# Two attention layers: the next batch's input is requested before the store and load of the second key group

## The chip, the cores and the metric

The kernel runs on one core of a Trainium2 chip. The time is the device time of one launch in microseconds (us). Lower is better. The engines are TensorE (PE in the profile, its weight loads PEld), VectorE (DVE), ScalarE (ACT), GpSimd (POOL) and SyncE (SP). SP only issues DMAs here, in program order, and all of the kernel's DMAs are issued by it.

## The reference

The input x is 8 batches of 256 channels by 32 x 32 positions (1024 tokens), float32. Two layers follow one another:

```
xn  = (x - mean_c(x)) / sqrt(var_c(x) + 1e-5) * gamma     # layer norm over the 256 channels
q, k, v = split(w_qkv @ xn)                               # 8 heads of 32 rows
a   = softmax(q^T k * 32^-0.5 + bias[head])               # 1024 x 1024 for each head
x1  = w_out @ (v a^T) + x                                 # end of layer 0
f, g, h = Wf @ x1 + bf, Wg @ x1 + bg, Wh @ x1 + bh        # f, g of 32 rows, h of 256
out = gamma1 * (h softmax(f^T g)) + x1                    # end of layer 1
```

The bias is a table over relative positions that a small network computes once.

## The kernel before

The program is written engine by engine, with semaphores between the engines. The Python functions only unroll it. For each of the 8 batches `b` there are two groups `g` of four heads, and each group has two phases.

- **Rows** (32 steps, `A_TILES`): PE makes a 128 x 1024 tile of the scores (lines 622 and 623), DVE adds the bias and finds the row maximum (line 1066), ACT takes the exponential and its row sum (line 840). Only the sums are kept.
- **Columns** (32 steps, `SN`): PE makes the scores again, turned round and with the row shifts folded in as two more rows of the operands (line 643), DVE adds the bias (1080), ACT takes the exponential (857), and PE multiplies with v (670).

Beside these steps runs all the rest, by tables of (step, kind, argument): `side_0` for the rows of group 0, `column_0` for its columns, and so on. An entry is done by each engine right behind its main work of that step, so an engine that waits in such an entry holds up its next tiles too. On PE row tiles are issued from step 3 on (`LEAD`), each ahead of its step's entries.

In the rows of group 0 of batch b the entries hold, in this order: the q of group 1 (steps 3 to 8), v (4 to 11), the k of group 1 (steps 11 to 16: four products on PE at line 446, `high_k` on ACT at 745, `low_k` on DVE at 945), the output projection of the batch before (513, 963), and then the layer norm of batch b + 1:

- step 18 `sum_x` on POOL (line 877): adds the two channel halves of xn into the buffer `st`;
- steps 22 and 23 `mean` on PE (line 460), a product of `st` with a constant matrix; step 23 `centre` on DVE (937); step 24 `square` on ACT (728), into `st`; step 25 `sum_squares` on POOL (880);
- steps 28 and 29 `var` on PE (line 460 again), step 30 `rstd` on ACT (737), and `norm` on POOL (886) in the columns that follow.

The buffer `st` (128 x 2 x 1024) is shared. It holds the q or k that has just been split in a high and a low part, until SP has stored it to DRAM (`through_dram`, line 338), from where it is loaded in another layout (lines 351 and 365). So `sum_x` waits for two things (lines 875 and 876): the second store of k of this batch has landed (`k_stored`), and x of the next batch has landed in `xn` (`x_loaded`). x can be requested only when the old xn has been read to the end, by v (`v_mm`) and by the products of k (`qk_mm`).

What SP issues in one batch is in the function `element` at line 403: q store and loads of group 1 (404, 405), k store and loads of group 1 (406, 407), x of the next batch (412), the shift rows (`shift_to_stack`), k and q of the next batch's group 0, the result of the batch before and this batch's x for the residual.

Of the kernel before, what the change touches and what calls it, by code (L numbers as in the profile page):

```python
# [25 lines left out]
def two_layer_attention(nc, x, gamma, w_qkv, w_out, w0, b0, w1, b1, w2, b2,  # L26
# [24 lines left out]
    with ExitStack() as ctx:  # L51
# [133 lines left out]
        def need(eng, name, b, n):  # L185
            value = b * per_batch[name] + n
            if value > 0:
                eng.wait_ge(SEMS[name], value)
# [111 lines left out]
        def split(g, t, half=NHALF - 1):  # L300


            return (1 - t) * NHALF + half + 1 if g == 0 else 2 * NHALF + t + 1
# [4 lines left out]
        def _(sp):  # L308
# [28 lines left out]
            def through_dram(dram, store_sem):  # L337
                sp.dma_start(dram.ap().rearrange("l h d n -> (h d) l n"), st[:].bitcast(F32)).then_inc(store_sem, 16)

            def q_out(b, g):  # L340
                need(sp, "lo_ready", b, split(g, 0))
                need(sp, "q_loaded", b, g * Q_DMAS)
                through_dram(q_dram, q_stored)

            def q_in(b, g, done):

                need(sp, "q_stored", b, 16 * (g + 1))
                need(sp, *done)
                for r, part in enumerate((0, 0, 1)):
                    for half in range(NHALF):  # L350
                        sp.dma_start(q_stack[r * HD:(r + 1) * HD, g, half].bitcast(F32),
                                     q_dram.ap()[part, :, :, half * HALF:(half + 1) * HALF]
                                     .rearrange("h d n -> d h n")).then_inc(q_loaded, 16)

            def k_out(b, g):
                need(sp, "lo_ready", b, split(g, 1))
                need(sp, "k_loaded", b, g * K_DMAS)
                through_dram(k_dram, k_stored)

            def k_in(b, g):  # L360

                need(sp, "k_stored", b, 16 * (g + 1))
                need(sp, "s_mm", b - 1, (g + 1) * SN)
                for r, part in enumerate((0, 1, 0)):
                    sp.dma_start(k_stack[r * HD:(r + 1) * HD, g].bitcast(F32),
                                 k_dram.ap()[part].rearrange("h d n -> d h n")).then_inc(k_loaded, 16)

            def shift_to_stack(b, g, r):

                need(sp, "rows_ready", b, g * NHALF + r + 1)  # L370
                for part in range(2):
                    sp.dma_start(q_stack[KS + part:KS + part + 1, g, NHALF - 1 - r].bitcast(F32)
                                 .rearrange("p h (t n) -> p (h t) n", n=P),
                                 shift_rows[part * HM:(part + 1) * HM, r, :].bitcast(F32)).then_inc(rows_loaded, 16)

            def residual_in(b):
                need(sp, "y_stored", b, 0)
                sp.dma_start(x1[:], x_dram[b]).then_inc(res_loaded, 16)

            def result_out(b):  # L380
                need(sp, "y_ready", b, KC * NHALF)
                sp.dma_start(out_dram[b], x1[:]).then_inc(y_stored, 16)
# [20 lines left out]
            def element(b, first, last):  # L403
                q_out(b, 1)
                q_in(b, 1, ("s_mm", b, 0))
                k_out(b, 1)
                k_in(b, 1)
                if not last:

                    need(sp, "v_mm", b, NT)  # L410
                    need(sp, "qk_mm", b, split(1, 1))
                    sp.dma_start(xn[:], x_dram[b + 1]).then_inc(x_loaded, 16)
                for r in range(NHALF):
                    shift_to_stack(b, 0, r)
                if not last:
                    k_out(b + 1, 0)
                    k_in(b + 1, 0)
                for r in range(NHALF):
                    shift_to_stack(b, 1, r)
                if not first:  # L420
                    result_out(b - 1)
                if not last:
                    q_out(b + 1, 0)
                    q_in(b + 1, 0, ("s_mm", b, SN))
                residual_in(b)

            batches(element)
            result_out(B - 1)
            sp.wait_ge(y_stored, 16 * B)
# [715 lines left out]
```

## Time and profile before

| | |
|---|---|
| median of 3 runs | 1933.42 us (1932.26 to 1933.76) |
| the profiled execution | 1937.73 us |
| its span, first to last instruction | 1935.6 us |
| PE / DVE / ACT / POOL busy | 84% / 78% / 72% / 4% |
| mean granted TensorE clock | 0.896 of full speed |
| chain that ended last | PE 46%, DVE 22%, issue 15%, DMA 8%, ACT 4%, SPq 3%, POOL 2% |

The span is cut by no pause between batches. From the second on, the batches last some 222 us each, and PE, DVE and ACT are all busy most of the time. In a timeline row the bracket at the end gives how long the engine had been idle before the row and what ended that wait. In a row of waits the numbers are the total, the count and the longest.

### The profile page before, as it was taken

How to read it: one execution, taken by the hardware profiler on the slowest of the kernel's cores; microseconds unless marked ns; L12 is line 12 of the kernel's file. 1: busy time of each engine (PE TensorE's matmuls, PEld its weight loads, DVE VectorE, ACT ScalarE, POOL GpSimd, SP SyncE). 2: the span in 40 equal slices, each digit the busy share in tenths (PEclk: the TensorE clock that was granted, in tenths of full speed). 3: DMA queues.
4: the chain of work that ended last, by engine and by line, in shares of the span. 5: the costliest groups of instructions: out<-in, count | busy, mean ns of one | idle time of the engine just before them, and what ended most of it. 6: DMA issues, size and time to landing. Idle time of an engine off the chain costs nothing.

```text
span 1935.6 us, 18745 instructions
## 1 busy us (share of the span) xinstructions
PE 1628.7 (84%) x5969; PEld 764.5 (39%) x5969; DVE 1508.7 (78%) x2201; ACT 1388.3 (72%) x2043; POOL 75.6 (4%) x36
## 2 busy tenths in 40 slices
PE   6644889789996899969997899959997899989988
PEld 2121333434443354424434354423534344434424
DVE  5334789679896898869896898868896898999863
ACT  1133788668785788858885787857886688888853
POOL 1100100010000000010000100010000100000000
PEclk8566778989998899979998899979998899999999
DMA  1396022402034021512034020421034010330010
GB/s 55 60 218 170 1 55 77 131 1 55 1 121 109 1 55 49 149 33 55 1 99 131 1 55 23 141 66 47 10 99 131 1 55 11 121 78 1 1 44 22
DMA packets 59029, 122.46 MB, mean 63 GB/s; under 512 B 22506, under 2 KB 25130, under 8 KB 58922
## 3 DMA queue, kind: packets, MB, share of 16 engines
q1 hardware_dynamic: 58932, 121.28, 22.9%
q8 instruction: 47, 0.77, 0.2%
q14 instruction: 50, 0.41, 0.1%
HBM read 78.66 MB, written 44.13 MB: 63 GB/s over the span
## 4 chain that ended last, share of the span: by engine, by line
PE 46%; DVE 22%; issue 15%; DMA 8%; ACT 4%; SPq 3%; POOL 2%; DVEq 0%; POOLq 0%; ACTq 0%
DVE biased L1066 11%; PE psum L643 9%; PE psum L568 9%; PE psum L670 7%; DVE biased L1080 5%; PE psum L622 5%; DMA xn<-in_x_dram 4%; PE psum L623 3%; PE psum L446 3%; PE psum L491 3%; PE psum L460 2%; ACT biased L840 2%; DMA k_parts<-st 2%; PE psum L525 2%; PE psum L501 1%
## 5 line engine op out<-in xcount | busy, mean ns | idle before, releaser
L1066 DVE CUSTOM_DVE_ANT_0 biased<-psum,bias_lines_sb 128x1024 f32<-128x1024 f32 x512 | 617.1, 1221 | 253.7 <-PE psum L623 211.8
L840 ACT ACTIVATE biased<-biased,nmax 128x1024 f32<-128x1024 f32 x512 | 587.3, 1147 | 245.0 <-DVE nmax L1066 241.3
L1080 DVE TENSOR_TENSOR biased<-psum,bias_lines_sb 128x1024 f32<-128x1024 f32 x512 | 597.9, 1218 | 53.6 <-PE psum L643 39.6
L857 ACT ACTIVATE probs<-biased 128x1024 f32<-128x1024 f32 x512 | 536.3, 1056 | 142.9 <-DVE biased L1080 120.6
L643 PE MATMUL psum<-q_stack,k_stack 98*128 98x512 f32 x1024 | 400.2, 499 | 36.3 <-DVE nmax L1066 16.1
L622 PE MATMUL psum<-k_stack,q_stack 96*128 96x512 f32 x512 | 339.3, 663 | 94.2 <-DVE nmax L1066 52.7
L643 PEld LDWEIGHTS psum<-q_stack,k_stack 98*128 98x128 f32 x1024 | 182.7, 205 | 328.2 <-DVE biased L1080 153.9
L670 PE MATMUL psum<-probs,vT 128*32 128x512 f32 x2048 | 283.1, 623 | 6.1 <-DVE st L955 3.9
L622 PEld LDWEIGHTS psum<-k_stack,q_stack 96*128 96x128 f32 x512 | 103.5, 202 | 286.1 <-DVE nmax L1066 177.5
L623 PE MATMUL psum<-k_stack,q_stack 96*128 96x512 f32 x512 | 216.1, 422 | 0.0
L568 PE MATMUL psum<-probs 128*128 128x512 f32 x384 | 186.6, 592 | 0.0
L460 PE MATMUL psum<-st,mean_w 128*128 128x512 f32 x64 | 56.8, 994 | 93.7 <-POOL st L877 78.4
L623 PEld LDWEIGHTS psum<-k_stack,q_stack 96*128 96x128 f32 x512 | 105.9, 207 | 53.6 <-issue 49.7
L491 PE MATMUL psum<-xn,wqkvT 128*128 128x512 f32 x128 | 76.3, 690 | 26.8 <-DVE st L949 15.2
L840 ACT ACTIVATION_READ_ACCUMULATOR biased<-biased,nmax 128x1 f32 x512 | 96.2, 188 | 0.0
L568 PEld LDWEIGHTS psum<-probs 128*128 128x128 f32 x384 | 72.6, 189 | 46.3 <-issue 36.1
L670 PEld LDWEIGHTS psum<-probs,vT 128*32 128x32 f32 x2048 | 42.6, 109 | 102.4 <-issue 75.5
L877 POOL TENSOR_TENSOR st<-xn 128x1024 f32<-128x1024 f32 x8 | 18.7, 2338 | 1240.0 <-DMA xn<-in_x_dram 1240.0
L446 PE MATMUL psum<-xn,wqkvT 128*128 128x512 f32 x128 | 67.1, 606 | 0.0
L788 ACT ACTIVATE probs<-probs,nmax 128x1024 f32<-128x1024 f32 x48 | 54.9, 1144 | 16.0 <-DVE probs L1012 15.2
L501 PE MATMUL psum<-wqkvT,xn 128*128 128x256 f32 x256 | 65.7, 378 | 0.0
L537 PE MATMUL psum<-whT,x 128*128 128x256 f32 x256 | 65.5, 380 | 0.0
(86 smaller groups left out, 1267.8 us busy)
## 6 DMA issues: line engine op xcount, KB each, us to landing
k_stack<-k_parts SPq DMA_DIRECT2D x48, 512.0 KB, 7.3
q_stack<-q_parts SPq DMA_DIRECT2D x96, 256.0 KB, 5.7
k_parts<-st SPq DMA_DIRECT2D x16, 1024.0 KB, 3.9
q_parts<-st SPq DMA_DIRECT2D x16, 1024.0 KB, 3.9
xn<-in_x_dram SPq DMA_DIRECT2D x8, 1024.0 KB, 11.2
x<-in_x_dram SPq DMA_DIRECT2D x8, 1024.0 KB, 9.2
out_dram<-x SPq DMA_DIRECT2D x8, 1024.0 KB, 4.1
bias_lines_sb<-bias_lines SPq DMA_DIRECT2D x32, 240.0 KB, 23.4
```

The source lines that it names most:

```text
L446: mm = pe.matmul(psum[0:rows, bank + half, :], lhsT(k), src[:, k, half * HALF:(half + 1) * HALF], start=(k == 0), stop=(k == KC - 1))
L460: mm = pe.matmul(psum[:, 6 + arg, :], mean_w[:], src[:, arg * HALF:(arg + 1) * HALF], start=True, stop=True)
L491: mm = pe.matmul(psum[:, bank, :], wqkvT[:, k, t * C:t * C + P], xn[:, k, half * HALF:(half + 1) * HALF], start=(k == 0), stop=(k == KC - 1))
L568: mm = pe.matmul(psum[:, 4 + 2 * c + half, :], hs[:, t % HS, c * P:(c + 1) * P], attn1[t % 3][:, half * HALF:(half + 1) * HALF], start=(t ...
L622: pe.matmul(psum[:, bank, :], lhsT, back(keys, 0, HALF, N), start=True, stop=True)
L623: pe.matmul(psum[:, bank + 1, :], lhsT, back(keys, HALF, HALF, N), start=True, stop=True).then_inc(SEMS["a_mm"], 1)
L643: mm = pe.matmul(psum[:, bank + i, :], k_stack[:, g, 2 * j + i, t * P:(t + 1) * P], q_stack[:, g, NHALF - 1 - half, 2 * j + i, ::-1], star ...
L670: mm = pe.matmul(psum[h * HD:(h + 1) * HD, 4 + half, :], vT[:, t, (g * HG + h) * HD:(g * HG + h + 1) * HD], probs[:, ((q - PV_LAG) * HP + ...
L840: nc.scalar.activation(biased[:, m % BIASED, :], biased[:, m % BIASED, :], ACT.Exp, scale=-1.0, bias=nmax[:, m:m + 1], accum_out=rowsum[:, ...
L857: nc.scalar.activation(probs[:, n % P_SLOTS], biased[:, n % BIASED, :] .rearrange("p (i n) -> p i n", i=2), ACT.Exp).then_inc(SEMS["probs_ ...
L1066: nc.vector.tensor_tensor_reduce(biased[:, m % BIASED, :], pair(bank_of(g, first, ("rows", m))), bias_lines[:, g * HG + h, a0:a0 + N], -1. ...
L1080: nc.vector.tensor_tensor(biased[:, n % BIASED, :].rearrange("p (i n) -> p i n", i=2), psum[:, bank:bank + 2, :], bias_lines[:, g * HG + 2 ...
```

## The change

SP's order in `element` changes, and nothing else: the request for the next batch's x, with the two waits that belong to it, moves ahead of the store and the loads of the second group's k.

```diff
             def element(b, first, last):
                 q_out(b, 1)
                 q_in(b, 1, ("s_mm", b, 0))
-                k_out(b, 1)
-                k_in(b, 1)
                 if not last:

                     need(sp, "v_mm", b, NT)
                     need(sp, "qk_mm", b, split(1, 1))
                     sp.dma_start(xn[:], x_dram[b + 1]).then_inc(x_loaded, 16)
+                k_out(b, 1)
+                k_in(b, 1)
                 for r in range(NHALF):
                     shift_to_stack(b, 0, r)
```

PE, DVE, ACT and POOL have the same instructions in the same order. On SP, this is the piece of the second batch, where `st` is the shared buffer, `q_parts` and `k_parts` are the copies in DRAM and `q_stack` and `k_stack` the operands of the scores. Before:

```order
L338 DMA q_parts<-st 128x2x1024
L351 DMA q_stack<-q_parts 32x4x512 x6
L338 DMA k_parts<-st 128x2x1024
L365 DMA k_stack<-k_parts 32x4x1024 x3
L412 DMA xn<-in_x_dram 128x2x1024
L372 DMA q_stack<-shift_rows 1x16x128 x4
```

The same piece of SP's order after the change:

```order
L338 DMA q_parts<-st 128x2x1024
L351 DMA q_stack<-q_parts 32x4x512 x6
L410 DMA xn<-in_x_dram 128x2x1024
L338 DMA k_parts<-st 128x2x1024
L365 DMA k_stack<-k_parts 32x4x1024 x3
L372 DMA q_stack<-shift_rows 1x16x128 x4
```

The x of the next batch has moved past one store and three loads of k, 4 DMAs. It happens 7 times, once in each batch but the last.

## Rows read from the trace of the kernel before

**Rows 1.** Waits of all engines: in total, times, longest, in us.
```profile
PE psum L460 <- POOL st L877: 78.4, 7, 15.8
```
**Rows 2.** Timeline of SP in the second batch: start, us, engine, line, operation.
```profile
357.74 2.69 SPq L351 DMA_DIRECT2D q_stack<-q_parts  x6
367.06 0.38 SPq L338 DMA_DIRECT2D k_parts<-st  x1
370.96 1.25 SPq L365 DMA_DIRECT2D k_stack<-k_parts  x3
372.31 0.39 SPq L412 DMA_DIRECT2D xn<-in_x_dram  x1
375.25 47.84 SPq L372 DMA_DIRECT2D q_stack<-shift_rows  x4
```
**Rows 3.** Timeline of the other engines in the same batch.
```profile
360.43 1.02 PE L446 MATMUL psum<-xn,wqkvT 128*128 128x512 f32 x2
...
375.34 0.40 PE L623 MATMUL psum<-k_stack,q_stack 96*128 96x512 f32 x1
...
383.59 2.34 POOL L877 TENSOR_TENSOR st<-xn 128x1024 f32<-128x1024 f32 x1 [166.88 <-DMA xn<-in_x_dram]
...
386.07 2.04 PE L460 MATMUL psum<-st,mean_w 128*128 128x512 f32 x2 [10.34 <-POOL st L877]
...
389.12 1.23 DVE L1066 CUSTOM_DVE_ANT_0 biased<-psum,bias_lines_sb 128x1024 f32<-128x1024 f32 x1 [12.00 <-PE psum L623]
...
390.71 2.35 DVE L937 TENSOR_TENSOR xn<-xn,psum 128x1024 f32<-128x1024 f32 x2 [0.36 <-PE psum L460]
...
399.86 1.12 PE L460 MATMUL psum<-st,mean_w 128*128 128x512 f32 x2 [2.21 <-POOL st L880]
...
457.62 0.47 PE L622 MATMUL psum<-k_stack,q_stack 96*128 96x512 f32 x1 [0.68 <-DVE biased L1080]
```
**Rows 4.** DMA view of 357.5 to 385.5 us, 40 slices of 0.7 us.
```profile
GB/s 0 32 240 301 199 152 255 211 211 234 211 193 9 0 41 415 427 421 193 0 41 234 246 217 211 205 205 211 240 228 199 199 328 410 433 157 7 0 0 0
```
**Rows 5.** SP's timeline around the residual's x, and that load's time to landing.
```profile
549.90 2.69 SPq L351 DMA_DIRECT2D q_stack<-q_parts  x6
552.64 0.43 SPq L378 DMA_DIRECT2D x<-in_x_dram  x1
...
DMA to landing us min/median/max: 9.2/9.2/9.2
```
**Rows 6.** First batch, timeline of SP, and of PE before its wait.
```profile
157.90 2.69 SPq L351 DMA_DIRECT2D q_stack<-q_parts  x6
160.69 0.38 SPq L338 DMA_DIRECT2D k_parts<-st  x1
169.56 1.25 SPq L365 DMA_DIRECT2D k_stack<-k_parts  x3
...
168.02 0.63 PE L623 MATMUL psum<-k_stack,q_stack 96*128 96x512 f32 x1
```
**Rows 7.** Last batch, timeline of PE in the rows.
```profile
1710.66 1.02 PE L446 MATMUL psum<-x,wfgT 128*96 128x512 f32 x2
...
1711.76 0.40 PE L623 MATMUL psum<-k_stack,q_stack 96*128 96x512 f32 x1
1711.99 1.02 PE L446 MATMUL psum<-x,wfgT 128*96 128x512 f32 x2
```
**Rows 8.** Seventh batch, timeline of PE and DVE behind the wait.
```profile
1497.44 2.04 PE L460 MATMUL psum<-st,mean_w 128*128 128x512 f32 x2 [10.56 <-POOL st L877]
...
1501.67 2.35 DVE L937 TENSOR_TENSOR xn<-xn,psum 128x1024 f32<-128x1024 f32 x2
```
**Rows 9.** Stretches: length, busy PE, PEld, DVE, ACT, POOL, granted clock, DMA share, GB/s.
```profile
386.00:392.00 6.00, 5.93 (x10) 3.09 (x11) 2.52 (x4) 1.24 (x2) 0.00 (x0) 0.52 0.00 0
...
404.00:428.00 24.00, 18.95 (x57) 8.09 (x57) 19.22 (x23) 15.15 (x22) 4.69 (x2) 0.72 0.00 1
```
**Rows 10.** DMA issues: count, KB each, median us to landing.
```profile
bias_lines_sb<-bias_lines SPq DMA_DIRECT2D x32, 240.0 KB, 23.4
```

## The prediction

> **What bounds the kernel now.** I read the page first: PE, DVE and ACT are each busy for 70 to 85% of the span, so no engine alone sets the time, and something must make them all wait together. The view of waits names it. PE sat idle in front of line 460, for POOL's line 877, seven times, 78.4 us in total and 15.8 at the longest [rows 1]. That leaves 62.6 us for the other six, 10.4 each. Seven is the number of batches that have a next one.
>
> Then the timeline of one such wait, in the second batch. PE ends its last row tile at 375.34 + 0.40 = 375.74 and does nothing until `mean` at 386.07. DVE's next tile comes at 389.12 after 12.00 us of idleness [rows 3]. Nothing on the core computes in between but POOL, whose `sum_x` starts at 383.59 and was released by the DMA of x. So the wait is on the path of every engine: what is taken from it is taken from the time.
>
> SP's timeline tells why x is so late. It stores k at 367.06, waits for the store until 370.96, issues three loads of k, and only then, at 372.31, requests x [rows 2], though x needed only the last product of k, which PE ended at 360.43 + 1.02 = 361.45 [rows 3]. The DMA view shows the second half of the delay. From about 371.5 on, 1.5 MB of k loads run at 200 to 240 GB/s, and only in the last three slices, from about 380, do x's bytes move at 410 to 430 [rows 4]. x's own megabyte needs 2.5 us. The rest is what stands ahead of it.
>
> **The change part by part.** *x is requested earlier.* SP ends the q loads at 357.74 + 2.69 = 360.43 and then waits for the last product of k, so x goes out at about 361.5 instead of 372.31, 10.8 us earlier. It queues behind the q loads, as the residual's x does in every batch: there x is issued right behind the same six loads, and lands 552.64 + 9.2 - 549.90 = 11.9 us after the first of them was issued [rows 5]. So x lands at 357.74 + 11.9 = 369.7, where it was about 383.5 before.
>
> *The k store is requested at the same time as before, behind x.* `low_k` on DVE gives its release, 367.06 as now. At that time x's megabyte is on its way: the q loads' bytes end near 365.9 [rows 4]. The question is whether the store waits for it. In the first batch the store was issued right behind the q loads and landed 169.56 - 157.90 = 11.7 us after the first of them [rows 6], against 370.96 - 367.06 = 3.9 with nothing ahead of it [rows 2]. Transfers on SP's queue therefore run one behind the other, and I let the store follow x: 11.9 + 1 MB at 420 GB/s (2.5) = 14.4 us after the first q load, which is 372.1. The near bound is 371.0 (no delay by x), the far one 14.4 + 5.0, that is 377.1, if x and the store each ran at the 210 GB/s of the loads [rows 4] instead of the 420 that both show now. I take 372.1, since each of the two has a row at 410 or more.
>
> *The wait changes its owner.* `sum_x` needs x and the store, and the store is now the later one, by 2.4 us. From `sum_x` to `mean` it is 386.07 - 383.59 = 2.5 us [rows 3], so `mean` can start at 372.1 + 0.1 + 2.5 = 374.7. PE comes there at 375.7. The wait is gone, with 1.0 us to spare, in six batches: 62.6 us. In the first batch the same sum gives 157.90 + 11.7 + 2.5 = 172.1 for the store and 174.7 for `mean`. PE comes there at 168.02 + 0.63 = 168.65 [rows 6], so it still waits 6.0 us of 15.8, and 9.8 are gained. Together 72.4 us.
>
> *What the idleness did to the clock.* Behind the wait the granted clock is 0.52, that is 1.2 GHz, from 386 to 392 [rows 9], and the two matmuls of the first `mean` take 2.04 us where two of the same form take 1.02 at full speed [rows 7]. From the start of `mean` to `centre` it takes 390.71 - 386.07 = 4.64 us in this batch and 4.23 in the seventh [rows 3, 8], 26.5 us over the six. At full speed: the row tile between the two means ends 1711.76 + 0.40 - 1710.66 = 1.5 us after the first began, the second mean 1711.99 + 1.02 - 1710.66 = 2.35 after it [rows 7], DVE does the tile first, 1.5 + 0.1 + 1.2 = 2.8, and then `centre`. Without the ten idle microseconds PE has been busy up to `mean`, so I take full speed: 26.5 - 6 x 2.8 = 9.7 us more. The bounds are 0 (the clock falls anyway) and those 9.7. In the first batch I count nothing, since 6 us of idleness stay.
>
> The Trainium skill says in "TensorE: Matmul & The Clock Gate", section "Part 1: The HAM clock gate (the "warmup" mystery)", that an idle stretch puts the array at half its clock, until it has been busy again. By that rule this term stands, and rows 9 agree (0.52 behind the wait).
>
> *From `centre` on* nothing changes. `var` comes 9.15 us after it (399.86), and PE waits 2.2 us for POOL there [rows 3]. That chain runs through DVE, ACT and POOL and stays, with its 2.2 us.
>
> *What is moved back.* The three k loads go out about 1.2 us later, 372.2 instead of 370.96, now without x behind them. PE's first tile with these keys is at 457.62 [rows 3], over 70 us later, so they are covered. The shift rows are issued at 375.25 in both cases [rows 2], and had 1.5 MB of k and 1 MB of x ahead of them. Now they have only k. They are needed when the columns begin, after `var`, so they are covered too. The sum is 72.4 + 9.7 = 82.1 us. The profiled execution goes from 1937.73 to about 1855.6. It stood 4.3 us above the median of the runs, so the median comes to 1933.4 - 82.1 = 1851.3.
>
> The Trainium skill has a rule that speaks against the change, in "DMA: Bandwidth & Descriptors", section "Queues, rings and completion order": on each DMA engine descriptors are consumed in ring order, and a DMA's semaphore increment lands only after every earlier write of that engine. By it the k store cannot be reported before x has landed, whatever its own pace. Rows 6 agree with its first half (11.7 us against 3.9). It makes the store the last thing that `sum_x` waits for; the sum above has that already, and without the rule `sum_x` would be released 1.1 us earlier with no gain for PE.
>
> **The rivals.** *A: the store takes the place of x as the wait.* If both megabytes run at 210 GB/s, the store lands at 377.1, `mean` starts at 379.7 and PE waits 4.0 us in six batches and 5 us more in the first, 29 us in all: 1880. Against it: no lone 1 MB transfer in rows 4 is that slow. For it: before, x and a store never followed one another. 8%.
>
> *B: the clock falls in spite of it.* PE has gaps of up to a microsecond ahead of `mean`, since it waits for DVE. If they are enough, the 9.7 us stay lost: 1861. 11%.
>
> *C: the slow stretch of the columns goes too.* From 404 to 428 the clock is 0.72, so PE spends 56% of it at 1.2 GHz, and DVE is busy for 19.2 of the 24 us [rows 9]. At full speed at most 4.8 us could go, say 3 in each of six batches, 18 us: 1833. For it: the long wait stands 18 us ahead of that stretch. Against it: it also follows `var`'s wait of 2.2 us, which stays. 11%.
>
> *D: slower.* The k store held up behind x so long that `sum_x` starts later than it did. It decides from 383.6 on, plus 1.6 for the clock, that is when the store takes over 18 us from its issue. The slowest transfers of the trace are the bias loads with 23.4 us to landing, with many megabytes ahead of them [rows 10]. With that figure the store lands at 390.5, `mean` is 7 us later than now, and seven batches cost 49 us: 1982. Against it: ahead of the store there are 2.5 MB, which rows 5 show to be through in 11.9 us. 2%.
>
> *E: x isn't earlier.* If SP's wait for the products of k ended late, or another engine read the old xn, nothing would move: 1933. The end of the last product at 361.45 [rows 3] speaks against it. 2%.
>
> **How the numbers follow.** The forecast, 1851, has 66%, with a range of its own from 1844 to 1859 (a microsecond in each batch either way). For 8 in 10 I reach to B and halfway to C: 1838 to 1866. Outside are A, D, E and most of C, 20% or a little less. About 0.2%, 4 us, can be told from no change. All cases but D and E are faster by more: 0.96. E is the same, 0.02, and D is slower, 0.02.
>
> **What would show it.** In the new profile: x requested right behind the q loads, about 1 us after their last issue, and landing near 369.7 on the old scale; the k store with 5 us to landing instead of 3.9, as its bytes follow x's; `sum_x` released by the k store and not by x; PE's waits in front of line 460 for line 877 down from 78.4 to 6 us, all in the first batch; the granted clock near 1.0 from `mean` to `centre`; the wait for line 880 unchanged at 2.2 us a batch; the batch 12 us shorter. The prediction is wrong if waits for line 877 stay above 2 us in the later batches (A), if the clock at `mean` is still 0.5 (B), or if a wait as long as the old one turns up behind `var`.

## The result, and the profile after

The changed kernel takes 1855.86 us (median of 4 runs, 1853.71 to 1856.92) beside 1933.59 for the kernel before (4 runs). The ratio is 0.9595, with a 95% interval from 0.9578 to 0.9612. That is 77.7 us less, where 82.1 were forecast (1851, range 1838 to 1866). The profiled execution went from 1937.73 to 1856.92, 80.8 us less.

First, who waits for `sum_x`, from the view of line 877. It answers to rows 1; a row holds us in total and the count.

```profile
its engine sat idle before it (us, times) until:
  DMA k_parts<-st: 1158.8, 7
  DMA xn<-in_x_dram: 5.4, 1
who waited for it (us, times):
  PE psum L460: 6.4, 2
```

POOL's releaser has changed: in all seven batches it is now the k store, `k_parts<-st`, where it was x. PE's wait in front of `mean` fell from 78.4 us [rows 1] to 6.4.

SP's timeline of the second batch, which answers to rows 2. The last line is the time from the request for this x to its landing, from the view of line 410:

```profile
346.86 2.69 SPq L351 DMA_DIRECT2D q_stack<-q_parts  x6
350.64 0.39 SPq L410 DMA_DIRECT2D xn<-in_x_dram  x1
356.18 0.38 SPq L338 DMA_DIRECT2D k_parts<-st  x1
361.41 1.27 SPq L365 DMA_DIRECT2D k_stack<-k_parts  x3
364.36 1.15 SPq L372 DMA_DIRECT2D q_stack<-shift_rows  x2
...
DMA to landing us min/median/max: 8.2/8.2/8.2
```

The q loads are on the queue 10.9 us earlier than before, so 357.74 there is 346.86 here. x is requested 1.1 us behind their last issue and lands 8.2 us later, at 358.8, which is 12.0 us after the first q load. The k store lands 361.41 - 356.18 = 5.2 us after its own request instead of 3.9, 14.55 us after the first q load and 2.6 us behind x. The DMA view from 346.5 to 374.5 us, in 40 slices of 0.7 us, shows why; it answers to rows 4:

```profile
GB/s 0 18 117 334 219 181 231 211 202 222 234 219 217 181 410 427 416 427 415 421 141 0 59 164 234 228 205 234 211 187 222 246 157 102 22 0 0 0 0 23
```

After the q loads at some 220 GB/s there are six and a half slices at 410 to 427 without a break, some 4.5 us and 1.9 MB. These are most of x and then the store; the first of x's bytes moved while q was still loading. The k loads come last.

The other engines in the same batch, which answer to rows 3:

```profile
361.46 2.37 POOL L877 TENSOR_TENSOR st<-xn 128x1024 f32<-128x1024 f32 x1 [155.90 <-DMA k_parts<-st]
...
364.45 0.40 PE L623 MATMUL psum<-k_stack,q_stack 96*128 96x512 f32 x1
...
364.69 1.02 PE L460 MATMUL psum<-st,mean_w 128*128 128x512 f32 x2
...
367.48 2.35 DVE L937 TENSOR_TENSOR xn<-xn,psum 128x1024 f32<-128x1024 f32 x2
...
376.63 1.13 PE L460 MATMUL psum<-st,mean_w 128*128 128x512 f32 x2 [2.21 <-POOL st L880]
```

`sum_x` ends at 363.83, 0.9 us before PE comes to `mean`, which starts right behind the row tile. From `mean` to `centre` it takes 2.79 us instead of 4.64, and from `centre` to `var` 9.15 as before. PE's wait in front of `var` has stayed at 2.2 us.

The clock in the 6 us from `mean` on (columns as in rows 9):

```profile
364.70:370.70 6.00, 5.00 (x15) 2.35 (x13) 5.61 (x7) 3.26 (x6) 0.00 (x0) 1.00 0.91 185
```

It is at 1.00, that is 2.4 GHz, where it was 0.52 [rows 9], and DVE is busy for 5.6 of the 6 us.

### The profile page after: what moved, and what is told of

Its sections match the earlier page's. It is cut to its first block, busy times and chain, and to the rows that moved or that the text cites. A ratio compares the mean times of both kernels' runs of the same rounds, so it can differ in the third digit from the quotient of the medians.

```text
span 1854.8 us, 18745 instructions
## 1 busy us (share of the span) xinstructions
PE 1617.7 (87%) x5969; PEld 757.5 (41%) x5969; DVE 1508.8 (81%) x2201; ACT 1389.4 (75%) x2043; POOL 75.7 (4%) x36
## 4 chain that ended last, share of the span: by engine, by line
PE 49%; DVE 24%; issue 16%; ACT 4%; DMA 3%; SPq 2%; POOL 1%; DVEq 0%; ACTq 0%
DVE biased L1066 12%; PE psum L643 9%; PE psum L568 9%; PE psum L670 8%; PE psum L622 5%; DVE biased L1080 5%; PE psum L623 4%; PE psum L446 3%; PE psum L491 3%; ACT biased L840 2%; PE psum L525 2%; PE psum L501 1%; SPq L390 1%; PE psum L460 1%; DMA q_parts<-st 1%
## 5 line engine op out<-in xcount | busy, mean ns | idle before, releaser
L622 PE MATMUL psum<-k_stack,q_stack 96*128 96x512 f32 x512 | 331.4, 647 | 95.3 <-DVE nmax L1066 55.1
L622 PEld LDWEIGHTS psum<-k_stack,q_stack 96*128 96x128 f32 x512 | 101.1, 197 | 285.3 <-DVE nmax L1066 184.3
L623 PE MATMUL psum<-k_stack,q_stack 96*128 96x512 f32 x512 | 213.8, 418 | 0.0
L623 PEld LDWEIGHTS psum<-k_stack,q_stack 96*128 96x128 f32 x512 | 103.7, 203 | 49.7 <-issue 46.1
L513 PE MATMUL psum<-o,woutT 128*128 128x512 f32 x128 | 64.4, 593 | 0.8 <-ACT o L809 0.8
```

The source lines that it names most:

```text
L622: pe.matmul(psum[:, bank, :], lhsT, back(keys, 0, HALF, N), start=True, stop=True)
L623: pe.matmul(psum[:, bank + 1, :], lhsT, back(keys, HALF, HALF, N), start=True, stop=True).then_inc(SEMS["a_mm"], 1)
```

## The experiments

The theory in parts: (1) x waited for the k loads and for the k store, since SP's queue runs in order; (2) the idle PE lost its clock and restarted slowly; (3) in the changed kernel the k store is what `sum_x` waits for, with under 1 us to spare. The rivals: only the moment of the request counts, or the slow start has nothing to do with PE's idleness, or the store's place on the queue doesn't matter.

### x between the k store and the k loads

```diff
+                k_out(b, 1)
                 if not last:
                     need(sp, "v_mm", b, NT)
                     need(sp, "qk_mm", b, split(1, 1))
                     sp.dma_start(xn[:], x_dram[b + 1]).then_inc(x_loaded, 16)
-                k_out(b, 1)
                 k_in(b, 1)
```

> Only half of the move: x is requested behind the k store and ahead of the three k loads. Theory (what stood ahead of x was the k loads' 1.5 MB and the wait for the store; on SP's queue transfers follow one another, so x and the store end together at the same time in either order): x is requested at 367.5 on the scale of the kernel before, lands about 2.5 us behind the store's 371.0, at 373.5, mean can start at 376.1 and PE waits 0.5 us in six batches: 3 us slower than the changed kernel, about 1859, with sum_x released by x. Rival (what counts is how early x is requested): the request comes only 4.8 us earlier than before instead of 10.8, so 4.8 us of each wait go, 7 x 4.8 = 34 us, about 1900.

Measured: 1875.67 us (5 runs, 1872.94 to 1878.12), ratio to the kernel before 0.9699 (0.9684 to 0.9713). Neither number was right: 19.8 us slower than the changed kernel instead of 3, and 24 us faster than the rival said. Three rows of this run's timelines, of SP, POOL and PE:

```profile
352.95 0.38 SPq L338 DMA_DIRECT2D k_parts<-st  x1
...
360.80 2.36 POOL L877 TENSOR_TENSOR st<-xn 128x1024 f32<-128x1024 f32 x1 [158.46 <-DMA xn<-in_x_dram]
...
363.31 2.05 PE L460 MATMUL psum<-st,mean_w 128*128 128x512 f32 x2 [1.69 <-POOL st L877]
```

`sum_x` starts 7.85 us after the store's request. The sum had 6.5: 3.9 for the store and 2.5 for x behind it. So PE waits 1.7 to 2.1 us in six batches instead of 0.5 (17.6 us in all with the first batch, 11.2 more than in the changed kernel). But that is half the loss. The first of the two products of `mean` takes 2.05 us instead of 1.02 (one matmul of the program stands as two, x2, in these rows), and the stretch behind has the low clock:

```profile
363.20:369.20 6.00, 5.89 (x9) 3.06 (x10) 2.48 (x4) 2.31 (x4) 0.00 (x0) 0.51 0.62 128
```

From `mean` to `centre` it took 4.1 to 4.6 us in these six batches, 26.8 us in sum against 16.8 in the changed kernel: 10.0 more. A wait of some 2 us costs as much again in the slow start. Together 21.2 us, against 17.1 in the spans and 19.8 in the medians. Most of the difference to the spans is that this execution came to its first row tile 3.1 us earlier, at 117.66 instead of 120.72, before anything of the change is due.

### The same, with PE kept busy in the short wait

```diff
                         need(pe, "lo_ready", b - 1, split(1, 1))
+                        if b > 0:
+                            for _ in range(2):
+                                pe.matmul(psum[:, 6, :], mean_w[:], wqkvT[:, 0, 0:HALF], start=True, stop=True)
                         need(pe, "x_summed", b, 1)
```

> The kernel with x requested between the k store and the k loads, in which PE waited 1.6 to 2.1 us ahead of mean and then took 4.1 to 4.6 us from mean to centre, with two extra matmuls on constants (1.7 us) ahead of each wait. Theory (that short wait alone lets the clock fall, and costs as much again in the slow start): with PE busy in it the clock stays up, mean to centre is 2.8 us, 10 us less in the six batches: about 1866 beside 1875.7. Rival (the slow start comes with x's late landing or with the traffic of the k loads beside it, not with PE's idleness): 1875 or more.

Measured: 1867.04 us (5 runs, 1865.03 to 1868.22), ratio 0.9636 (0.9623 to 0.9650) against 0.9699 without the two matmuls. The intervals are apart, and SP's order is the same in both. PE and DVE in the second batch (the extra line moves `mean` to 463 and `centre` to 940):

```profile
366.71 1.88 PE L458 MATMUL psum<-wqkvT,mean_w 128*128 128x512 f32 x4
368.54 1.12 PE L463 MATMUL psum<-st,mean_w 128*128 128x512 f32 x2
...
371.43 2.35 DVE L940 TENSOR_TENSOR xn<-xn,psum 128x1024 f32<-128x1024 f32 x2
```

`mean` to `centre` is 2.9 us here and in the other five batches, 17.3 us in sum instead of 26.8. By the ratios the run is 12 us faster than the one without the two matmuls, by the medians of two groups of runs 8.6, and 10 were expected. The work that PE does is useless, and the kernel gets faster by it. The slow start belongs to PE's idleness and not to the traffic.

### The kernel before, with PE kept busy in the long wait

The same lines with 20 matmuls, in the kernel before:

> The kernel before with its old order and its old waits, but PE runs 20 matmuls of 128x512 on constants (into the bank that mean overwrites) ahead of each of the seven waits for sum_x, some 9 us of work inside a wait of 10.4. The result isn't touched. Theory (the term for the clock): the wait for x stays until the same time, but the granted clock stays at its upper level, mean to centre takes 2.8 us instead of 4.2 to 4.6 in six batches, 9.7 us in all: about 1924 beside 1933.5 for the kernel before. Rival (the slow start behind the wait isn't paid in time, or has another cause than PE's idleness): 1933.5, with 0.5 of the clock behind the wait or with 4.4 us from mean to centre.

Measured: 1967.65 us (4 runs), ratio 1.0176 (1.0160 to 1.0192). The dose was wrong. I had counted 9 us for 20 of them, but each took 0.87 us (it stands as two records, x40 for 20), and together they ran longer than the wait:

```profile
375.18 17.33 PE L458 MATMUL psum<-wqkvT,mean_w 128*128 128x512 f32 x40
...
384.67 2.34 POOL L880 TENSOR_TENSOR st<-xn 128x1024 f32<-128x1024 f32 x1 [168.62 <-DMA xn<-in_x_dram]
392.35 1.02 PE L463 MATMUL psum<-st,mean_w 128*128 128x512 f32 x2
...
395.13 2.35 DVE L940 TENSOR_TENSOR xn<-xn,psum 128x1024 f32<-128x1024 f32 x2
```

`sum_x` was ready at 387.0 and `mean` came at 392.35. The time says nothing about the clock, but the rows do: 2.78 us from `mean` to `centre`. With 11 of them:

> The kernel before, as in the run with 20 extra matmuls, but with 11 of them ahead of each wait for sum_x. A matmul of 128x512 with its two passes took 0.87 us there (17.3 us for 20), so 11 take 9.5 us and end about 1 us before mean is released at the wait's usual 10.4; the wait itself isn't lengthened. Theory (the term for the clock): the clock stays up, mean to centre takes 2.8 us instead of 4.2 to 4.6 in six batches, 9.7 us in all: 1924 beside 1934 for the kernel before. Rival (the extra work makes the core as slow as the idleness did, or the slow start is hidden by a later wait): 1934.

Measured: 1930.59 us (5 runs, 1927.37 to 1932.18) beside 1937.89 for the kernel before in that group, ratio 0.9966 (0.9953 to 0.9979). The second batch:

```profile
384.28 1.13 PE L463 MATMUL psum<-st,mean_w 128*128 128x512 f32 x2 [1.18 <-POOL st L880]
...
387.18 2.35 DVE L940 TENSOR_TENSOR xn<-xn,psum 128x1024 f32<-128x1024 f32 x2
```

PE still waits, 0.4 to 1.8 us in the six batches, and `mean` to `centre` is 2.9: 26.5 - 17.4 = 9.1 us less over the six, and 7.3 in the medians. The interval of the ratio reaches from 4 to 9 us, and 9.7 were expected. So the clock was worth some 7 to 9 us of the change, with the long wait left in place.

### One more megabyte ahead of the k store

```diff
                     sp.dma_start(xn[:], x_dram[b + 1]).then_inc(x_loaded, 16)
+                    sp.dma_start(spare_dram.ap()[b], x_dram[b + 1]).then_inc(spare_stored, 16)
                 k_out(b, 1)
```

> The changed kernel with one more transfer ahead of the k store: a copy of the same 1 MB of x from DRAM to an unused DRAM tensor, 7 times. Theory (SP's queue runs in order, and sum_x now waits for the k store): the store lands 2.5 us later if the copy runs at 420 GB/s, 5 us at 210, against 0.8 us of slack, so PE waits 1.7 to 4.2 us in six batches and 2.5 to 5 more in the first: 13 to 30 us slower than the changed kernel, 1868 to 1886, with the store's time to landing up from 5.2 us. Rival (the store isn't held by what stands ahead of it, or has several us to spare): 1856.

Measured: 1879.06 us (4 runs, 1877.66 to 1881.83), ratio 0.9716 (0.9702 to 0.9729), 23.2 us slower than the changed kernel. The timelines of SP, POOL and PE in the second batch (lines 340 and 367 are the store and the k loads):

```profile
351.53 0.39 SPq L412 DMA_DIRECT2D xn<-in_x_dram  x1
351.96 0.59 SPq L413 DMA_DIRECT2D spare<-in_x_dram  x1
357.07 0.38 SPq L340 DMA_DIRECT2D k_parts<-st  x1
364.52 1.27 SPq L367 DMA_DIRECT2D k_stack<-k_parts  x3
...
364.57 2.37 POOL L881 TENSOR_TENSOR st<-xn 128x1024 f32<-128x1024 f32 x1 [157.45 <-DMA k_parts<-st]
...
367.08 1.52 PE L464 MATMUL psum<-st,mean_w 128*128 128x512 f32 x2 [1.34 <-POOL st L881]
```

The copy goes to a DRAM tensor that nobody reads. The store takes 7.4 us to land instead of 5.2; less the 0.9 us to spare, that leaves PE's wait of 1.3. Over the batches the delay is 2.2 to 3.2 us. PE waits 19.6 us in front of `mean` instead of 6.4, 13.2 more, and `mean` to `centre` took 26.0 us over the six batches instead of 16.8, 9.2 more. The sum, 22.4, is the difference of the spans (1877.4 - 1854.8 = 22.6). So what stands ahead of the store on the queue counts, and what it had to spare was under 2.2 us.

### The q loads behind the k store

What x and the store still queue behind are the six q loads, which nobody needs before the second group begins.

```diff
                 q_out(b, 1)
-                q_in(b, 1, ("s_mm", b, 0))
                 if not last:
...
                 k_out(b, 1)
+                q_in(b, 1, ("s_mm", b, 0))
                 k_in(b, 1)
```

> The changed kernel with the six q loads of group 1 moved behind the request for x and the k store, so that SP's order is q store, x, k store, q loads, k loads. Theory (the q loads' 1.5 MB are what x and the store still queue behind): x lands about 5 us after its request, the store 4 us after its own, sum_x starts 1 to 2 us earlier in the later batches, where nothing waits for it any more, and the 6.2 us that PE still waits in the first batch go, with 1.4 us for the clock there: about 1848. Rival (3 MB of loads now stand ahead of the shift rows, which the columns need some 20 us later): the shift rows land late and PE waits at the first tile of the columns instead, 1856 or slower.

Measured: 1847.13 us (4 runs, 1844.94 to 1849.49), ratio 0.9549 (0.9536 to 0.9562), 8.7 us less than the changed kernel. In the first batch, SP and PE:

```profile
146.34 0.39 SPq L409 DMA_DIRECT2D xn<-in_x_dram  x1
157.81 0.36 SPq L338 DMA_DIRECT2D k_parts<-st  x1
158.22 4.04 SPq L351 DMA_DIRECT2D q_stack<-q_parts  x6
162.97 1.25 SPq L365 DMA_DIRECT2D k_stack<-k_parts  x3
...
158.97 0.79 PE L622 MATMUL psum<-k_stack,q_stack 96*128 96x512 f32 x1 [8.90 <-DVE nmax L1066]
...
165.97 1.91 PE L460 MATMUL psum<-st,mean_w 128*128 128x512 f32 x2
...
186.15 0.71 PE L643 MATMUL psum<-q_stack,k_stack 98*128 98x512 f32 x2 [0.70 <-DVE nmax L1066]
```

PE no longer waits for `sum_x` in any batch, so the 6.2 us of the first batch are gone, and most of the gain is there. Its columns begin at 186.15 instead of 194.10, but this execution came to its first row tile 2.6 us earlier, at 118.08 instead of 120.72, so 5.3 us of the 7.95 belong to the edit, and the 8.7 of the medians may hold some luck of this kind.

Two parts of what was expected did not come. In the first batch the slow start stayed (3.98 us from `mean` to `centre`, the first product 1.91), though no wait stood right ahead of it: PE had idled for 8.90 us before 158.97, and the granted clock was 0.50 from there to 165.9. And in the second batch `sum_x` begins 10.82 us after the request for x, exactly as in the changed kernel, and in the later ones after 10.7 to 10.8 instead of 10.6 to 11.9. x lands sooner, 4.8 us after its request instead of 8.2 and before the store is even requested, but the store still takes 5.2 us and not 4, now with the q loads right behind it. The shift rows came in time: no wait for a DMA stands in front of line 643.

### The same, with `var` one step later

```diff
-        side_0 += [(28, "var", 0), (29, "var", 1), (30, "rstd", 0)]
+        side_0 += [(29, "var", 0), (30, "var", 1), (31, "rstd", 0)]
```

> The kernel with the q loads last, and in the table of side work of the rows var goes from steps 28 and 29 to 29 and 30, and rstd from 30 to 31. PE then issues one more row tile (0.9 us at full speed) before it waits for sum_squares, where 2.2 us are lost in each of seven batches. Theory (that wait is on the path of PE and DVE): 0.9 to 1.5 us less in each of seven batches, 6 to 10 us: about 1839 beside 1847. Rival (the start of the columns is set by the chain mean, centre, square, sum_squares, var, rstd, which the one step lengthens): 1847 or slower.

Measured: 1836.35 us (4 runs, 1835.43 to 1839.81), ratio to the kernel before 0.9484 (0.9471 to 0.9497), below the interval of the version without the edit. PE in the second batch:

```profile
368.27 0.50 PE L622 MATMUL psum<-k_stack,q_stack 96*128 96x512 f32 x1
...
370.38 1.12 PE L460 MATMUL psum<-st,mean_w 128*128 128x512 f32 x2 [1.38 <-POOL st L880]
```

One more row tile stands ahead of `var`, and the wait is 1.38 us instead of 2.2. PE's waits there are 8.8 us over seven batches, where the changed kernel and the version without the edit have 15.4. This is the fastest version, 19.5 us below the changed kernel and 10.8 below the version without the edit by the medians of two groups of runs. 6 to 10 were expected.

The shorter wait alone does not account for that, since part of what the rival said came too. PE now waits for `rstd` ahead of the third column tile, 9.9 us over seven batches, where it was 0.7 without the edit:

```profile
378.34 1.09 PE L643 MATMUL psum<-q_stack,k_stack 98*128 98x512 f32 x2 [1.48 <-ACT o L737]
```

What else differs is the clock. In the 24 us from just ahead of the first column tile it is 0.79 in the changed kernel and 0.85 here (sixth batch of each; in the second both have 0.79):

```profile
1220.53:1244.53 24.00, 19.29 (x66) 7.99 (x66) 20.75 (x24) 16.36 (x23) 4.69 (x2) 0.79 0.01 1
...
1207.48:1231.48 24.00, 17.88 (x61) 7.12 (x60) 20.11 (x23) 16.47 (x22) 4.68 (x2) 0.85 0.01 1
```

How much of the gain is the wait and how much the clock was not separated.

## Why the prediction was right

**The wait.** Forecast: 62.6 us in six batches and 9.8 in the first, 6.0 left there. Measured: 78.4 to 6.4, of which 6.2 in the first batch and 0.2 in the seventh. Right, by the mechanism that was named.

**The change of owner.** Forecast: x lands 11.9 us after the first q load and the k store 14.4, 2.4 us behind x, with 1.0 us to spare for PE. Measured in the second batch: 12.0 and 14.55, and 0.9 to spare. In the first batch, where 172.1 and 174.7 were forecast for the store and `mean`, they came at 172.06 and 174.60. The store took 5.0 to 5.8 us in batches two to six. In the seventh it took 6.3 and the spare time was gone, which is the 0.2 us above. The run with one more megabyte showed that it is the store, and what stands ahead of it, that matters. Rival A had the right mechanism, and the two rates of 420 GB/s kept it out: the two ran at 410 to 427 in sum and landed 2.6 us apart. Its price, 1880, was too low, though: it counts PE's waits of 4 us and leaves out the slow start behind them. Waits of 1.25 us and more brought it back in the runs, so it would have been up to 9.7 us more, 1890.

**The clock.** Forecast: 26.5 us from `mean` to `centre` over six batches become 16.8. Measured: 16.8 (2.79 us in five batches, 2.86 in the seventh). The runs with PE kept busy show the cause from both sides. Rival B is refuted for this kernel. But its point, that small gaps might do, was nearer than it was given: in the run with x between store and loads a wait of 1.7 us was enough, and in the run with one more megabyte 1.25. The same gaps of 0.5 to 0.8 us ahead of `mean` without such a wait left the clock at 1.00 in all six batches of the changed kernel.

**What hung on nothing.** The k loads and the shift rows went out later or with less ahead of them, and no new wait appeared. `var`'s wait stayed at 15.4 us over seven batches, as forecast, and rival C's 18 us didn't come. The clock of that stretch is 0.79 in the six batches of the changed kernel, and it was 0.79 before in five of them; the 0.72 of the second batch, on which rival C was priced, was the exception. That `var`'s wait is what holds it down fits the last run (0.85 in five of six batches with 1.4 us of wait), but isn't shown by it alone.

**The size.** The profiled executions differ by 80.8 us where 82.1 were summed. Up to the last k store (1699.98 before, 1617.58 after) the gain was 82.4 us, and from there to the end, where neither kernel does anything different, the changed one took 237.2 us instead of 235.6. The rest of the miss, 77.7 against 80.8, is no step of the kernel: I took it that both profiled executions stand 4.3 us above their medians. The one of before stood 4.1 above, the one of after only 1.1. A sum made on one execution carries such a difference.

## What to carry to other kernels

Where several engines idle together behind a transfer, look at what stands ahead of it on its queue. If the bytes ahead are wanted later than it is, change places, and count which of the transfers is the last one then. A short wait on TensorE can cost twice its length, since the slow restart is paid on top: an order that leaves 1.8 us of wait gave back 20 of 78 us. So the last two microseconds of such a wait are worth as much care as the first eight. And loads that nobody awaits yet can go behind those that somebody does.

## What the runs showed of the hardware

- After an idle stretch of 1.6 to 2.1 us on PE, with gaps of 0.5 to 0.8 us ahead of it, the granted clock of the next 6 us was 0.50 to 0.54 in four batches and 0.72 in two. With the same stretch filled by 1.9 us of matmuls it was 1.00 and the first `mean` took 1.12 us instead of 2.05. After waits of 0.4 to 1.8 us that followed 9.6 us of dense matmuls it was 1.00 too. So what the engine did before the wait counts, and not the wait's length alone. I had expected only the long wait to cost the clock.
- Two 1 MB transfers, x and then the k store, ran at 410 to 427 GB/s in sum, while the q and k loads moved at some 220 GB/s. A copy from DRAM to DRAM of 1 MB ahead of the store delayed it by 2.2 to 3.2 us.
- With the store first and x behind it, the pair took 7.85 us to `sum_x`, against 6.5 expected, and the store itself 4.9 instead of 3.9. With x requested right behind it, x doesn't simply wait its turn. With the q loads right behind it the store took 5.2 us, though x had landed before. So what is issued behind a transfer can delay it as well as what is ahead. Why wasn't tried.
